# Two transformer layers on one core: V's high and low parts in one stationary tile, row sums spread by DMA, and an earlier place for the head products in cross-attention

## The chip, the core and the metric

The kernel runs on one core of one Trainium2 chip. Its engines work side by side, each through its own queue in order, and wait for each other through semaphores: TensorE (PE; matrix products into the eight PSUM banks, and transposes as products with the identity), VectorE (DVE), ScalarE (ACT), GpSimd (POOL), and SyncE (SP), which here issues every DMA. The metric is device time in microseconds. Lower is better.

## What is computed

A first layer (a gated state update with attention over a context) makes `x`, and a second layer, where most of the time goes, has three phases over 8 batches of 256 rows of 256 columns:

```python
h = layernorm(x, ln1_g, ln1_b)
x = attention(h, h, a1_Wq, a1_Wk, a1_Wv, a1_Wo, a1_bo) + x          # self
h = layernorm(x, ln2_g, ln2_b)
x = attention(h, context, a2_Wq, a2_Wk, a2_Wv, a2_Wo, a2_bo) + x    # cross, 120 rows of context
h = layernorm(x, ln3_g, ln3_b)
p = h @ ff_Wp + ff_bp
u, gate = jnp.split(p, 2, axis=-1)
return u * gelu(gate) @ ff_Wo + ff_bo + x

def attention(x, ctx, Wq, Wk, Wv, Wo, bo):       # 16 heads of 64
    sim = einsum('bihd,bjhd->bhij', q, k) / 8
    out = einsum('bhij,bjhd->bihd', softmax(sim), v)
    return out @ Wo + bo
```

## The kernel before

**High and low parts.** Products run in the type `F32R`, which keeps fewer bits than float32. So each operand is kept as two tiles: a rounded high part (written by ScalarE or GpSimd) and the low part that is left (a subtraction, nearly always on VectorE). A product is then three: high x high, low x high, high x low. The helper `product` issues them (L1386 to L1388).

**Steps.** The two attention phases run in 128 steps, one per batch and pair of heads: G = 8b + i, with i from 0 to 7, b from 0 to 7 for self-attention and 8 to 15 for cross-attention. Both heads of a pair (e = 0, 1) are worked together. The order on each engine is written out by hand in `step_self` and `step_cross`, one of each per engine, and a pipeline runs through them:

- `scores(G + 1)` on TensorE; `row_max` on VectorE; `softmax_pair` on ScalarE (exponentials, with their row sums to `expsum`); `inverse_sums` on VectorE gives `rs`, one reciprocal per row and head.
- `transpose_p(G)` on TensorE: the unscaled exponentials `p`, transposed into banks 4 and 5; `round_pT` (ScalarE) and `pT_low` (VectorE) write their high and low parts.
- `weighted_values(G - 1)` on TensorE, into bank 6: V (stationary) times pT (moving). The tiles `v_hi` and `v_lo` hold per pair [head 0 | zeros | head 1] of 64 columns each, so that each head's 128-column window puts the other head's 64 output rows to zero and both heads add up in one 128 x 256 result. That is 2 heads x 3 products x 2 tiles of rows in self-attention (12), x 1 in cross-attention (6). GpSimd had written the zeros once (L544 ff.).
- The scale by the row sums: `widen_sums` (GpSimd, L566) repeats the reciprocals over 64 columns, TensorE transposes that in two instructions into bank 6's right half (L1663), `copy_rT` (ScalarE, L781) copies it to SBUF, and `normalise_o` (VectorE, L1178) multiplies. Only then is bank 6 free for the next step.
- `split_o` (GpSimd) makes high and low parts of the scaled result, and `project_out` multiplies eight pairs by Wo into bank 7.

Between these stand the projections of later steps (`project_self`, `project_keys`, `project_queries`, `project_values`), and on fixed steps the preparation of the next batch: statistics at i = 0, `xhat` at 1, the residual of the batch before at 2, transposing and splitting the input at 3. In cross-attention the next batch's context is transposed at the end of step 3 (`context`), split at the start of VectorE's step 4 (`context_low`), and used by `project_keys(b + 1, 0)` in TensorE's step 4. New weights come in units of 1024 columns, one per step: in batch 0, the last self batch (7), the first cross batch (8) and the last (15).

**The changed places on TensorE:** in cross-attention a step is `scores`, `transpose_p`, a projection, `weighted_values`, then the rest (L1807 ff.).

## Time and profile before

| | us |
|---|---|
| median of 3 runs | 1027.96 (1027.17 to 1029.55) |
| profiled execution | 1026.68 |
| its span | 1024.9 |
| mean granted TensorE clock | 0.981 |
| TensorE / VectorE / ScalarE / GpSimd busy | 981.0 / 704.5 / 624.1 / 366.3 |

The span is the time from the first to the last instruction of the profiled execution; its own time is 1.8 us longer. Until 164.6 us runs mainly the first layer, then self-attention to about 576.9, cross-attention to about 874, and the feed-forward to the end. A timeline row gives the start, then the duration (for several instructions in a row, that of all). Matmuls are pipelined: a product of 256 columns is shown with 0.28 us but the next starts before its end, so the spacing of starts tells what one costs. L-numbers are lines of the kernel.

### The profile page before, as it was taken

The page shows a single profiled execution, that of the slowest core. Times are in us where ns is not written, and L with a number is a line of the kernel's source. Part 1 is how long each engine was busy: PE and PEld are TensorE (multiplying, and loading weights), DVE is VectorE, ACT ScalarE, POOL GpSimd, SP SyncE. Part 2 cuts the span into 40 slices and gives each one's busy share as a digit, 9 for nine tenths or more (in the row PEclk, how much of TensorE's full clock was granted, in tenths as well). Part 3 has the DMA queues.
Part 4 walks back from the last instruction along what each step waited for, and adds up shares of the span by engine and source line. Part 5 has one row for each costly group of instructions (what it writes and reads, how often), then busy time and mean ns, then how long its engine had stood idle before and what let it go on. Part 6 is the DMA issues. An engine that isn't in the chain of part 4 may idle for free.

```text
span 1024.9 us, 21429 instructions
## 1 busy us (share of the span) xinstructions
PE 981.0 (96%) x7892; PEld 921.9 (90%) x7892; DVE 704.5 (69%) x1594; ACT 624.1 (61%) x1945; POOL 366.3 (36%) x514
## 2 busy tenths in 40 slices
PE   7799999999999999999999999999999997999998
PEld 6687877899999999999999989999999997999998
DVE  5577578767676767676778777667667667566674
ACT  5556457757575756565667676676666667433343
POOL 1222337433333333342423345455454545301010
PEclk9799899999999999999999989999999999999999
DMA  7311100104000000000003000200000001001010
GB/s 219 102 42 42 36 21 32 32 2 104 2 22 1 23 1 22 2 21 2 22 2 88 21 27 23 87 27 27 2 27 26 2 22 62 22 22 38 26 32 22
DMA packets 30445, 34.62 MB, mean 34 GB/s; under 512 B 4360, under 2 KB 23816, under 8 KB 30344
## 3 DMA queue, kind: packets, MB, share of 16 engines
q1 hardware_dynamic: 30344, 33.26, 10.7%
q8 instruction: 65, 1.06, 0.4%
q14 instruction: 36, 0.29, 0.1%
HBM read 24.86 MB, written 8.39 MB: 32 GB/s over the span
## 4 chain that ended last, share of the span: by engine, by line
PE 81%; DVE 8%; ACT 7%; issue 2%; POOL 1%; SPq 0%; DMA 0%; DVEq 0%; ACTq 0%
PE bank L1386 15%; PE bank L1388 14%; PE bank L1387 14%; PE bank L1647 8%; PE bank L1626 5%; PE bank L1403 5%; PE bank L1689 3%; PE bank L1691 3%; PE bank L1690 3%; PE bank L1663 3%; ACT p L769 2%; PE bank L1508 1%; PE bank L1509 1%; PE bank L1510 1%; DVE hT_lo L1142 1%
## 5 line engine op out<-in xcount | busy, mean ns | idle before, releaser
L577 POOL TENSOR_TENSOR oT_hi<-oT,ones 128x256 fp32r<-128x256 f32 x128 | 93.9, 733 | 362.7 <-DVE oT L1182 362.7
L769 ACT ACTIVATE p<-bank,negmax 128x256 f32<-128x256 f32 (+1 forms) x512 | 207.8, 427 | 20.2 <-DVE negmax L1159 15.9
L779 ACT CAST pT_hi<-bank 128x512 fp32r<-128x512 f32 (+1 forms) x256 | 110.7, 486 | 166.6 <-PE bank L1647 166.4
L1386 PE MATMUL bank<-hT_hi,w_hi 128*128 128x256 f32 x640 | 188.5, 295 | 3.9 <-DVE qkT_lo L1213 1.6
L1388 PE MATMUL bank<-hT_hi,w_lo 128*128 128x256 f32 x640 | 179.0, 280 | 0.0
L1387 PE MATMUL bank<-hT_lo,w_hi 128*128 128x256 f32 x640 | 178.9, 280 | 0.0
L1174 DVE TENSOR_TENSOR pT_lo<-bank,pT_hi 128x512 fp32r<-128x512 f32 (+1 forms) x256 | 129.6, 547 | 0.5
L1155 DVE TENSOR_REDUCE negmax<-bank 128x2 f32<-128x512 f32 x128 | 82.1, 683 | 66.9 <-PE bank L1626 66.9
L1386 PEld LDWEIGHTS bank<-hT_hi,w_hi 128*128 128x128 f32 x640 | 121.6, 190 | 7.0 <-issue 3.6
L1387 PEld LDWEIGHTS bank<-hT_lo,w_hi 128*128 128x128 f32 x640 | 121.4, 190 | 0.0
L1388 PEld LDWEIGHTS bank<-hT_hi,w_lo 128*128 128x128 f32 x640 | 121.0, 189 | 0.0
L1386 PE MATMUL bank<-pT_hi,v_hi 128*128 128x256 f32 (+1 forms) x384 | 119.4, 311 | 0.0
L769 ACT ACTIVATION_READ_ACCUMULATOR p<-bank,negmax 128x1 f32 x512 | 110.2, 215 | 0.0
L1647 PE MATMUL bank<-ident,p 128*128 128x128 f32 (+1 forms) x768 | 109.9, 280 | 0.0
L1387 PE MATMUL bank<-pT_lo,v_hi 128*128 128x256 f32 (+1 forms) x384 | 108.7, 283 | 0.0
L1388 PE MATMUL bank<-pT_hi,v_lo 128*128 128x256 f32 (+1 forms) x384 | 108.6, 283 | 0.0
L579 POOL TENSOR_TENSOR oT_lo<-oT,oT_hi 128x256 fp32r<-128x256 f32 x128 | 94.6, 739 | 10.0
L1647 PEld LDWEIGHTS bank<-ident,p 128*128 128x128 f32 (+1 forms) x768 | 84.6, 141 | 8.7 <-ACT p L769 0.3
L568 POOL TENSOR_TENSOR rsum_wide<-rsum,ones 128x256 f32<-128x256 f32 x128 | 79.8, 624 | 0.0
L873 ACT ACTIVATE p<-bank,params_pp 128x256 f32<-128x256 f32 x64 | 30.4, 475 | 78.4 <-PE bank L1388 78.3
L1387 PEld LDWEIGHTS bank<-pT_lo,v_hi 128*128 128x128 f32 (+1 forms) x384 | 73.7, 192 | 0.0
L1388 PEld LDWEIGHTS bank<-pT_hi,v_lo 128*128 128x128 f32 (+1 forms) x384 | 73.4, 191 | 0.0
(204 smaller groups left out, 2738.9 us busy)
## 6 DMA issues: line engine op xcount, KB each, us to landing
w_stage<-in_weights SPq DMA_DIRECT2D x47, 256.0 KB, 4.6
x_in<-x_dram SPq DMA_DIRECT2D x24, 256.0 KB, 2.9
x_dram<-x_out SPq DMA_DIRECT2D x16, 256.0 KB, 3.2
l_x<-in_x SPq DMA_DIRECT2D x4, 512.0 KB, 5.0
x_dram<-l_out SPq DMA_DIRECT2D x4, 512.0 KB, 2.8
out_dram<-x_out SPq DMA_DIRECT2D x8, 256.0 KB, 3.1
w_stage<-in_weights SPq DMA_DIRECT2D x9, 128.0 KB, 5.6
l_ctx<-in_ctx SPq DMA_DIRECT2D x4, 180.0 KB, 4.4
```

Source lines behind the costliest of these rows:

```text
L568: nc.gpsimd.tensor_tensor(rsw[:, G % 2, :, :].rearrange("p t (e d) -> p (t e) d", e=2), rs[:, G % 2, :].unsqueeze(2).broadcast_to([128, NT ...
L577: nc.gpsimd.tensor_tensor(oh[:, G % PAIRS, :], of[:, :], ones[:, :], ALU.mult).then_inc(y["o_hi"], 1)
L579: nc.gpsimd.tensor_tensor(ol[:, G % PAIRS, :], of[:, :], oh[:, G % PAIRS, :].bitcast(F32), ALU.subtract).then_inc(y["o_lo"], 1)
L769: last = nc.scalar.activation(p[:, G % 2, e, t * cols:(t + 1) * cols], scores_at(G, e, t), ACT.Exp, bias=negmax[:, G % 2, t, e:e + 1], acc ...
L779: nc.scalar.copy(pTh[0:r, G % 2, e, 0:n], bank[4 + e][0:r, 0:n]).then_inc(y["pT_hi"], 1)
L1155: nc.vector.tensor_reduce(negmax[:, G % 2, :, e], score_bank(G, e)[:, :].rearrange("p (t n) -> p t n", t=NT), AX.X, ALU.max, negate=True). ...
L1174: nc.vector.tensor_tensor(pTl[0:r, G % 2, e, 0:n], bank[4 + e][0:r, 0:n], pTh[0:r, G % 2, e, 0:n].bitcast(F32), ALU.subtract).then_inc(y[" ...
L1386: nc.tensor.matmul(dst, lh, rh, start=(i == 0), stop=False)
L1387: nc.tensor.matmul(dst, lh, rl, start=False, stop=False)
L1388: last = nc.tensor.matmul(dst, ll, rh, start=False, stop=(i == n - 1))
L1403: last = nc.tensor.matmul(dst, *((a, c) if weights_stay else (c, a)), start=(i == 0), stop=(i == 4))
L1647: last = nc.tensor.transpose(bank[4 + e][0:n, j * S + t * 128:j * S + (t + 1) * 128], p[:, G % 2, e, t * cols + j * 128:t * cols + j * 128 ...
```

## The change

1. **One V tile.** `v_hi_lo` holds per head 128 columns: head 0 as [high | low], head 1 as [low | high]. One stationary load gives both products with high and low V; with pT's high and low parts that is 2 products per head and tile in place of 3 (the product low x low is now in). The zeros and their memsets go.
2. **Two halves to add.** Each head now has its own 128 x 256 half of a bank, 64 rows of high-V and 64 of low-V results. ScalarE copies the low-V rows to `oT_low_values` in two instructions of 64 x 256 (`copy_low_values`, in place of `copy_rT`), and VectorE adds them to the others in two (`add_low_values`, in place of `normalise_o`).
3. **Sums by DMA.** `widen_sums`, its two transposes and the copy go. SyncE writes the 512 reciprocals of a step to DRAM in 8-byte pieces (`send_sums`) and one step later reads them back, each head's row to 64 partitions (`spread_sums`). GpSimd multiplies the sum of halves by them, ahead of its two splitting instructions. Rings of four (`DEEP`) hold `oT` and `rsumT`.
4. **SyncE's queue** is written step by step: sends and spreads, with `load`, `store`, `load_context` and the weight units at fixed steps between them. A row `x_in` is loaded two batches ahead, not three.
5. **Cross-attention's order.** On TensorE `weighted_values(G - 1)` moves ahead of `transpose_p(G)`; its result alternates between banks 2 and 6 (`o_bank`), and scores use two banks, not three. On ScalarE the copies stand ahead of `round_pT` and the exponentials, on VectorE the additions ahead of `pT_low`. Both heads' transposed exponentials share one bank, so `round_pT` and `pT_low` are one instruction each.

```diff
-VW = 3 * DH
+VW = 2 * DH
+DEEP = 4
...
         def score_bank(G, e):
-            return bank[(2 * G + e) % 3 if G < STEPS // 2 else G % 3]
+            return bank[(2 * G + e) % 3 if G < STEPS // 2 else G % 2]
+        def o_bank(G):
+            return bank[6 if G < STEPS // 2 or G % 2 else 2]
+        def pT_both(G):
+            return bank[4 + G % 2][0:SC, :].rearrange("p (e n) -> p e n", e=2)
...
+            def send_sums(G):
+                sp.wait_ge(y["rsum"], G + 1)
+                if G >= DEEP:
+                    sp.wait_ge(*spread_until(G - DEEP))
+                sp.dma_start(sums_dram[G % DEEP, :, :].rearrange("e (q t) -> q e t", t=NT),
+                             rs[:, G % 2, :].rearrange("q (e t) -> q e t", e=2)).then_inc(y[f"rsum_row{G % 2}"], 16)
+            def spread_sums(G):
+                sp.wait_ge(y[f"rsum_row{G % 2}"], 16 * (G // 2 + 1))
...
+                for e in range(2):
+                    sp.dma_start(rT[e * DH:(e + 1) * DH, G % DEEP, :],
+                                 sums_dram[G % DEEP, e:e + 1, :].partition_broadcast(DH)).then_inc(y[f"rT{G % 2}"], 16)
...
             def split_o(G):
+                pool.wait_ge(y["o_sum"], G + 1)
+                pool.wait_ge(*spread_until(G))
...
+                nc.gpsimd.tensor_tensor(on[:, :].rearrange("p (t q) -> p t q", t=NT),
+                                        of[:, G % DEEP, :].rearrange("p (t q) -> p t q", t=NT),
+                                        rT[:, G % DEEP, :].rearrange("p (q t) -> p t q", t=NT),
+                                        ALU.mult).then_inc(y["o_norm"], 1)
...
-            def copy_rT(G):
+            def copy_low_values(G):
                 act.wait_ge(y["o"], G + 1)
-                nc.scalar.copy(rT[:, :], bank[6][:, S:2 * S]).then_inc(y["rT_copied"], 1)
+                if G >= 2:
+                    act.wait_ge(y["o_sum"], G - 1)
+                nc.scalar.copy(ob[0:DH, G % 2, :], o_bank(G)[DH:128, 0:S])
+                nc.scalar.copy(ob[DH:128, G % 2, :], o_bank(G)[0:DH, S:2 * S]).then_inc(y["o_low"], 1)
...
             def inverse_sums(G):
                 dve.wait_ge(y["exp"], 2 * G + 2)
+                if G >= 2:
+                    dve.wait_ge(y[f"rsum_row{G % 2}"], 16 * (G // 2))
...
-            def normalise_o(G):
+            def add_low_values(G):
+                dve.wait_ge(y["o_low"], G + 1)
+                if G >= DEEP:
+                    dve.wait_ge(y["o_norm"], G - DEEP + 1)
+                nc.vector.tensor_tensor(of[0:DH, G % DEEP, :], o_bank(G)[0:DH, 0:S], ob[0:DH, G % 2, :],
+                                        ALU.add)
+                nc.vector.tensor_tensor(of[DH:128, G % DEEP, :], o_bank(G)[DH:128, S:2 * S], ob[DH:128, G % 2, :],
+                                        ALU.add).then_inc(y["o_sum"], 1)
...
             def weighted_values(G):
+                    pe.wait_ge(y["o_sum"], G if G < STEPS // 2 else G - 1)
                 pe.wait_ge(y["pT_lo"], 2 * G + 2)
                 pe.wait_ge(y["v_lo"], values_until(b, g))
-                product(bank[6][:, 0:S], terms).then_inc(y["o"], 1)
+                for e in range(2):
+                    dst = o_bank(G)[:, e * S:(e + 1) * S]
+                    for j in range(tiles):
+                        vs = vv[0:r, j, (2 * g + e) * VW:(2 * g + e + 1) * VW]
+                        pc = slice(j * S, (j + 1) * S)
+                        nc.tensor.matmul(dst, vs, pTh[0:r, G % 2, e, pc], start=(j == 0), stop=False)
+                        last = nc.tensor.matmul(dst, vs, pTl[0:r, G % 2, e, pc], start=False, stop=(j == tiles - 1))
...
                 if G + 1 < STEPS:
                     scores(G + 1)
+                weighted_values(G - 1)
                 transpose_p(G)
...
-                weighted_values(G - 1)
```

**Three places in the instruction order**, each before and after. TensorE, cross-attention, from the last score product of step 3 on. `p` are the exponentials, `w,cT` is `project_values`, `pT,v` is `weighted_values`. Before:

```order
L1388 MATMUL bank<-qkT_hi,qkT_lo 128x240
L1647 MATMUL bank<-ident,p 120x128 x4
L1403 MATMUL bank<-w_hi,cT_hi 120x512
L1403 MATMUL bank<-w_hi,cT_lo 120x512
L1403 MATMUL bank<-w_lo,cT_hi 120x512
L1403 MATMUL bank<-w_hi,cT_hi 120x512
L1403 MATMUL bank<-w_lo,cT_hi 120x512
L1663 MATMUL bank<-ident,rsum_wide 128x128 x2
L1386 MATMUL bank<-pT_hi,v_hi 128x256
L1387 MATMUL bank<-pT_lo,v_hi 128x256
L1388 MATMUL bank<-pT_hi,v_lo 128x256
```

After:

```order
L1446 MATMUL bank<-qkT_hi,qkT_lo 128x240
L1733 MATMUL bank<-pT_hi,v_hi_lo 128x256
L1734 MATMUL bank<-pT_lo,v_hi_lo 128x256
L1733 MATMUL bank<-pT_hi,v_hi_lo 128x256
L1734 MATMUL bank<-pT_lo,v_hi_lo 128x256
L1713 MATMUL bank<-ident,p 120x128 x4
L1461 MATMUL bank<-w_hi,cT_hi 120x512
L1461 MATMUL bank<-w_hi,cT_lo 120x512
L1461 MATMUL bank<-w_lo,cT_hi 120x512
L1461 MATMUL bank<-w_hi,cT_hi 120x512
L1461 MATMUL bank<-w_lo,cT_hi 120x512
```

The products of `weighted_values` now stand ahead of the transposes, four in place of six, and the two `rsum_wide` transposes are gone.

VectorE, cross-attention, all of step 3 and the start of step 4 up to `context_low` (`cT_lo`, and the second instruction on `cT_hi`). `xhat<-bank` is the scaled input of the next batch, `oT<-bank,rsumT` is `normalise_o`. Before:

```order
L1167 RECIPROCAL rsum<-expsum 128x4
L1159 TENSOR_REDUCE negmax<-bank 128x4
L1136 TENSOR_SCALAR xhat<-bank,params_pp 128x256 x2
L1174 TENSOR_TENSOR pT_lo<-bank,pT_hi 120x256 x2
L1142 TENSOR_TENSOR hT_lo<-xhat,hT_hi 128x512
L1219 TENSOR_TENSOR v_lo<-bank,v_hi 120x4x2x64
L1182 TENSOR_TENSOR oT<-bank,rsumT 128x256
L1167 RECIPROCAL rsum<-expsum 128x4
L1159 TENSOR_REDUCE negmax<-bank 128x4
L1147 TENSOR_TENSOR cT_lo<-bank,cT_hi 128x120
L1148 TENSOR_TENSOR cT_hi<-bank,cT_hi 64x120
```

After:

```order
L1216 RECIPROCAL rsum<-expsum 128x4
L1206 TENSOR_REDUCE negmax<-bank 128x4
L1183 TENSOR_SCALAR xhat<-bank,params_pp 128x256 x2
L1237 TENSOR_TENSOR oT<-bank,oT_low_values 64x256
L1239 TENSOR_TENSOR oT<-bank,oT_low_values 64x256
L1229 TENSOR_TENSOR pT_lo<-bank,pT_hi 120x2x256
L1189 TENSOR_TENSOR hT_lo<-xhat,hT_hi 128x512
L1277 TENSOR_TENSOR v_hi_lo<-bank,v_hi_lo 120x4x128
L1216 RECIPROCAL rsum<-expsum 128x4
L1206 TENSOR_REDUCE negmax<-bank 128x4
L1194 TENSOR_TENSOR cT_lo<-bank,cT_hi 128x120
L1195 TENSOR_TENSOR cT_hi<-bank,cT_hi 64x120
```

`normalise_o` at the end of the step became two additions ahead of `pT_lo`, which is one instruction now.

ScalarE, cross-attention, steps 3 and 4 up to the exponentials. Before:

```order
L779 CAST pT_hi<-bank 120x256 x2
L769 ACTIVATE p,expsum<-bank,negmax 128x120 x4
L757 CAST hT_hi<-xhat 128x512
L801 CAST v_hi<-bank 120x4x2x64
L783 COPY rsumT<-bank 128x256
L761 CAST cT_hi<-bank 128x240
L779 CAST pT_hi<-bank 120x256 x2
L769 ACTIVATE p,expsum<-bank,negmax 128x120 x4
L783 COPY rsumT<-bank 128x256
```

After:

```order
L829 COPY oT_low_values<-bank 64x256
L830 COPY oT_low_values<-bank 64x256
L822 CAST pT_hi<-bank 120x2x256
L809 ACTIVATE p,expsum<-bank,negmax 128x120 x4
L797 CAST hT_hi<-xhat 128x512
L848 CAST v_hi_lo<-bank 120x4x2x64
L801 CAST cT_hi<-bank 128x240
L829 COPY oT_low_values<-bank 64x256
L830 COPY oT_low_values<-bank 64x256
L822 CAST pT_hi<-bank 120x2x256
L809 ACTIVATE p,expsum<-bank,negmax 128x120 x4
```

The one copy late in a step became two at its head, so that the rounding of pT and the exponentials stand behind them.

## Rows read from the trace of the kernel before

**Rows 1.** the profile page, busy time, share of the span and instructions by engine

```profile
PE 981.0 (96%) x7892; PEld 921.9 (90%) x7892; DVE 704.5 (69%) x1594; ACT 624.1 (61%) x1945; POOL 366.3 (36%) x514
```

**Rows 2.** windows: length, busy us (instructions) by engine, clock, DMA; self, cross, last cross batch

```profile
319.10:370.50 51.40, 51.40 (x444) 47.60 (x443) 35.02 (x73) 32.80 (x101) 18.11 (x27) 1.00 0.04 12
703.20:739.90 36.70, 35.54 (x299) 34.59 (x298) 26.00 (x65) 24.72 (x100) 18.34 (x27) 1.00 0.06 19
838.00:874.00 36.00, 30.18 (x225) 28.72 (x224) 25.11 (x58) 23.89 (x91) 16.27 (x23) 0.91 0.14 45
```

**Rows 3.** timeline: start us, us, line; TensorE in a self-attention step

```profile
301.31 0.28 PE L1388 MATMUL bank<-hT_hi,w_lo 128*128 128x256 f32 x1
301.44 0.38 PE L1663 MATMUL bank<-ident,rsum_wide 128*128 128x128 f32 x2
...
301.77 0.28 PE L1387 MATMUL bank<-pT_lo,v_hi 128*128 128x256 f32 x1
301.89 0.28 PE L1388 MATMUL bank<-pT_hi,v_lo 128*128 128x256 f32 x1
```

**Rows 4.** timeline of TensorE, cross batch 11, steps 2 to 5

```profile
703.22 0.60 PE L1647 MATMUL bank<-ident,p 128*120 128x128 f32 x4
...
712.26 0.41 PE L1663 MATMUL bank<-ident,rsum_wide 128*128 128x128 f32 x2 [1.16 <-DVE oT L1182]
...
713.29 0.32 PE L1403 MATMUL bank<-cT_hi,w_hi 128*128 128x120 f32 x1
...
716.30 0.60 PE L1647 MATMUL bank<-ident,p 128*120 128x128 f32 x4
```

**Rows 5.** timeline of VectorE over the same steps

```profile
706.17 0.69 DVE L1213 TENSOR_TENSOR qkT_lo<-bank,qkT_hi 128x512 fp32r<-128x512 f32 x1 [0.70 <-ACT qkT_hi L797]
...
707.36 0.66 DVE L1159 TENSOR_REDUCE negmax<-bank 128x4 f32<-128x480 f32 x1
707.93 0.99 DVE L1136 TENSOR_SCALAR xhat<-bank,params_pp 128x256 f32<-128x256 f32 x2
708.83 0.75 DVE L1174 TENSOR_TENSOR pT_lo<-bank,pT_hi 120x256 fp32r<-120x256 f32 x2
710.07 1.11 DVE L1142 TENSOR_TENSOR hT_lo<-xhat,hT_hi 128x512 fp32r<-128x512 f32 x1 [0.49 <-ACT hT_hi L757]
711.11 0.68 DVE L1219 TENSOR_TENSOR v_lo<-bank,v_hi 120x512 fp32r<-120x512 f32 x1
711.71 0.41 DVE L1182 TENSOR_TENSOR oT<-bank,rsumT 128x256 f32<-128x256 f32 x1
712.04 0.16 DVE L1167 RECIPROCAL rsum<-expsum 128x4 f32<-128x4 f32 x1
712.12 0.62 DVE L1159 TENSOR_REDUCE negmax<-bank 128x4 f32<-128x480 f32 x1
712.66 0.27 DVE L1147 TENSOR_TENSOR cT_lo<-bank,cT_hi 128x120 fp32r<-128x120 f32 x1
```

**Rows 6.** groups by line and shape: busy us, mean ns | idle before, releaser

```profile
L577 POOL TENSOR_TENSOR oT_hi<-oT,ones 128x256 fp32r<-128x256 f32 x128 | 93.9, 733 | 362.7 <-DVE oT L1182 362.7
...
L783 ACT COPY rsumT<-bank 128x256 f32<-128x256 f32 x128 | 49.5, 386 | 7.0 <-PE bank L1388 1.1
...
L324 DVE TENSOR_TENSOR w_lo<-w_stage,w_hi 128x1024 fp32r<-128x1024 f32 x22 | 27.0, 1229 | 17.0 <-ACT w_hi L314 17.0
...
L792 ACT CAST qkT_hi<-bank 64x480 fp32r<-64x480 f32 x32 | 17.7, 554 | 12.7 <-PE bank L1403 12.5
```

**Rows 7.** DMA issues by tile: KB each, median us from issue to landing

```profile
w_stage<-in_weights SPq DMA_DIRECT2D x47, 256.0 KB, 4.6
...
ctx_in<-in_ctx SPq DMA_DIRECT2D x8, 30.0 KB, 3.2
```

**Rows 8.** windows around a fall of the granted clock

```profile
596.80:600.40 3.60, 1.36 (x11) 1.27 (x12) 3.56 (x10) 2.23 (x10) 1.35 (x2) 1.00 0.59 180
600.40:607.20 6.80, 6.80 (x34) 6.80 (x34) 3.47 (x8) 3.98 (x13) 2.72 (x5) 0.50 0.01 2
```

201 lines of the change are left out of this document (107 added, 94 removed).

## The prediction, made before the change was timed

> **What bounds the kernel now.** I read the busy times first: TensorE is busy 96% of the span, VectorE 69%, ScalarE 61%, GpSimd 36% [rows 1]. Then the same by batch in the two attention phases (eight head pairs, one step each; this is what repeats). A self-attention batch takes 51.5 us and TensorE is busy in all of it. A cross-attention batch takes 36.7 us with TensorE busy 35.5 [rows 2]. So self-attention is bound by TensorE instruction for instruction, and cross-attention nearly. Third, TensorE's own rows in a cross batch: the one place where it waits is for `normalise_o`, 1.16 us, ahead of the `rsum_wide` transposes at 712.26 [rows 4]. Fourth, VectorE's rows over the same stretch explain that wait: from step i = 2 to i = 4 it has a chain with hardly a gap, and `normalise_o` stands near its end [rows 5]. I write T2 for the start of `transpose_p` in step i = 2 (703.22), T5 for that of i = 5 (716.30), and so on.
>
> **Self-attention, TensorE.** Back-to-back products of 256 columns start 0.12 us apart. From the last projection (301.31) over the two `rsum_wide` transposes and the first V product to the second (301.77) it is 0.46 us, where two plain intervals would be 0.24 [rows 3]. So the two transposes cost 0.22. Each step loses them and 4 of its 12 V products, which ran in intervals of 0.118 (0.12 rounded up): 0.22 + 4 x 0.118 = 0.69 us, 5.5 per batch, 44 over 64 steps if all of it shows.
>
> Does VectorE keep up? A batch has 35.0 us of VectorE work [rows 2]. In place of one multiply per step (0.41 us) come two additions on 64 partitions. Half the partitions do not mean half the time: ScalarE takes 0.55 us for 64x480 and 0.39 for 128x256 [rows 6], so time goes by elements per partition. Back to back, an instruction starts some 0.08 us ahead of its forerunner's shown end (the multiply at 711.71 takes 0.41, the next starts at 712.04 [rows 5]), so one more adds 0.33: 37.7 us. With a wait of some 0.7 per step for ScalarE's rounding of q and k, as at 706.17 [rows 5], it is 43.3 against TensorE's new 51.5 - 5.5 = 46.0. It fits, narrowly: steps 2 and 3, which also carry the residual and the next batch's input, I expect to run 1 us late and to be caught up by step 5. ScalarE makes two copies of 0.39 in place of one, 0.31 more back to back, 2.5 per batch: from 32.8 to 35.3. GpSimd swaps its widening for a multiply, so that it has three instructions of 0.73 a step [rows 6], 17.6 of 46: hidden.
>
> The cover is gone where weights are converted: a unit costs VectorE 1.23 us [rows 6]. Batch 0 has three units, the last self batch six, which brings VectorE there to 43.3 + 7.4, about 51. I take a gain of 4 us for batch 0, 1.5 for the last and 5.5 for each of the six between: 38.5.
>
> **Cross-attention.** On TensorE each step loses 2 of 6 V products and the transposes: 0.22 + 2 x 0.118 = 0.46. With the V products ahead of `transpose_p`, and two output banks, the wait for `normalise_o` goes. What is late next is the context: `project_keys` of the next batch cannot start before VectorE has `cT_lo`. That came at the end of the chain from 706.17 (queries' low part) to 712.66 and its second half, and the keys followed at 713.29 [rows 4, 5]: 7.1 us.
>
> I worked this chain again in the new order, start to start from the same rows: queries' low 0.61, reciprocal 0.08, row maximum 0.57, scaled input 0.90, additions 0.66, pT low 0.60 (now one instruction, as large per partition as the v_lo row), input low 0.78 to 1.04, v low 0.60, reciprocal 0.08, maximum 0.54, context 0.55. That is 6.0 to 6.3 us. The two multiplies and the 0.49 us wait before `hT_lo` leave, two pairs of additions less one enter. But the chain begins 0.3 us later after T2, since ScalarE makes its two copies (0.7) ahead of the rounding, which used to start 0.42 after T2. Taking 6.2, the keys start 9.5 us after T2 instead of 10.1. Behind them stand 20 short products (713.29 to about 715.57: 2.3), the scores 0.55 and now the V products 0.55, then T5: 12.9 against 13.1 before. I take 0.3 gained in these three steps. TensorE sits idle in them in four pieces (at the values, the context, the V products, the keys), 2.7 us together, the longest 1.7.
>
> The other five steps are TensorE's own: 0.46 each in four, and 0.2 in step 1, where `project_queries` waits for `keys_low`, now later. Per batch 0.3 + 4 x 0.46 + 0.2 = 2.35. Six even batches give 14. The first, with two weight units in this very stretch, I take at 2; the last, where five units bind VectorE and ScalarE already (TensorE 30.2 of 36.0 [rows 2]), at 0.5. Cross-attention together 16.6.
>
> **The sums by DMA.** No row shows a transfer in 8-byte pieces, 256 to a step. The nearest are 30 KB in 256-byte pieces, 3.2 us to landing, and the 256 KB parts of weight units, 4.6 [rows 7]. With 3.2 the spread of pair G-1, issued about 1.4 us after the reciprocal of step G, lands at 4.6; GpSimd needs 2.2 more, 6.8; the tightest user, pair 7 in `project_out` of cross step 1, asks at about 7.9: 1.1 to spare. A landing time of 4.6 would eat 1.4: 0.3 us at step 1, 2 us in all. A gain it cannot be, since the transposes it replaces are already counted. I take 0, by the nearest row. VectorE's new wait (the reciprocal of G on the send of G-2) has two steps, 9 us; behind it queue the row maximum and with it the exponentials. Between the sends SyncE now has single loads and stores, each waiting for what was done a step before; only `store_first(3)` at G = 1 holds the next send, until GpSimd's last pass over the first layer, and pair 2's sum is not wanted before that pass is over. Cost 0.
>
> The Trainium skill speaks against this part: "DMA: Bandwidth & Descriptors", Specifications, has pieces under 512 B handled by read-modify-write, and its account of the fixed cost of about 2 us says that completion waits for the memory written, HBM worst. No row here shows such writes; by that page alone two trips of 2 us would still fit in the 4.6.
>
> **Edges.** The removed memsets stood on GpSimd beside a busy TensorE: 0. At the start of the feed-forward, pair 127's split has a third instruction ahead of `project_out`: 0.7 lost. And the clock. The granted clock is 1.00 in even batches [rows 2], but 0.50 (the 1.2 GHz level) from 600.4 to 607.2, right behind 3.6 us in which TensorE was busy 1.36 [rows 8]. The idle that I expect ahead of T5 comes close to that in some batches: I charge 2 us. The Trainium skill ("TensorE: Matmul & The Clock Gate", Part 1) has the clock set by how busy the array has lately been; the trace agrees at 600.4.
>
> **Sum.** 38.5 + 16.6 - 0.7 - 2 = 52.4. The profiled execution took 1026.7 us (span 1024.9 and 1.8 around it); the median shown, 1028.0, is 1.3 above. 1026.7 - 52.4 + 1.3 = 975.6. I say 975, its own range 966 to 985.
>
> **Rivals.**
> 1. TensorE binds everywhere: 64 x 0.69 + 64 x 0.46, and the wait of 1.2 in seven batches: 44 + 29 + 8 = 81, 947 us. For it: the busy share of 96%. Against it: VectorE's chain, whose parts are all in one queue. Chance 0.12.
> 2. Self-attention becomes bound by VectorE and ScalarE. If the lateness in steps 2 and 3 reaches `project_values(b, 3)`, which asks for `v_lo` within 0.1 us of when I have it, or additions cost more than 0.33, half of 38.5 is lost: 994 us. For it: 43.3 of 46.0 leaves little. Against: ScalarE's part of the wait shrinks when VectorE is late. Chance 0.14.
> 3. The clock falls in nearly every cross batch. A fall lasts 6.8 us at half speed [rows 8], of which waiting hides a part; at 2.4 us a batch the 16.6 are gone: 992 us. For it: idle of 2.7 us ahead of T5. Against: the present wait never did it in an even batch. Chance 0.12.
> 4. The sums' round trip binds, and it is slower than before. A send is waited for two steps later, so a send of L us forces steps of at least L/2. Steps now average 6.4 and 4.6 [rows 2]; with L = 12 cross steps take 6.0 (64 x 1.4 = 90 us more) and self-attention keeps some 28 of its gain: 1090 us. It turns the change into a loss from about L = 10.5, where cross steps lose 39. For it: 256 tiny writes, in no row. Against: nothing in [rows 7] is near. Chance 0.03.
>
> Forecast 0.59. The range 957 to 997 takes in rivals 2 and 3 at their price and stops short of 1 and 4. A measurement of this kernel tells 0.2%, 2 us, from no change: faster 0.95, same 0.02, slower 0.03.
>
> **What the profile after would show.** A self batch of 46.0 us with TensorE busy throughout; above 47 it is rival 2. A cross batch of 34.3, with TensorE waiting at `project_keys` for `cT_lo` and at the V products for `pT_lo`; 33 or less, or 36, and my chain is wrong. Granted clock 1.00 in even batches, else rival 3. Additions at 0.41 us, copies at 0.39. Sends landing within 5 us, and VectorE never waiting at the reciprocal, else rival 4.

## The result, and the profile after

The changed kernel takes **1004.68 us** (median of 4 runs, 1004.02 to 1005.22) against 1027.62 of the kernel before, run beside it: ratio 0.977 [0.976, 0.979]. I had forecast 975, between 957 and 997. The change is faster, by less than half of what I expected.

The busy times of the changed kernel; they answer to [rows 1]:

```profile
PE 931.9 (93%) x7252; PEld 864.4 (86%) x7252; DVE 768.2 (77%) x1658; ACT 672.5 (67%) x2009; POOL 388.3 (39%) x498
```

TensorE lost 49 us of work, 640 instructions, but the span lost only 21.9: TensorE now waits more. Where, by stretches of the span, T being the first `transpose_p` of a step:

| us | before | after | gained | forecast |
|---|---|---|---|---|
| to T of G = 0 | 164.6 | 163.9 | 0.6 | 0 |
| batch 0 | 51.3 | 50.9 | 0.4 | 4 |
| batches 1 to 6 | 51.54 each | 46.40 each | 30.9 | 33 |
| batch 7 (converts weights) | 51.8 | 55.6 | -3.8 | 1.5 |
| batch 8 | 43.0 | 41.2 | 1.8 | 2 |
| batches 9 to 14 | 36.67 each | 34.7 to 39.9 | -4.6 | 14.1, less 2 for the clock |
| batch 15, to T of G = 127 | 33.4 | 31.4 | 2.0 | 0.5 |
| from there to the end | 151.5 | 156.9 | -5.3 | -0.7 |

In the windows of the changed kernel (columns as in [rows 2]) the first row is a plain self batch, the second cross batch 9, the third cross batch 11, the fourth batches 9 to 14 together:

```profile
307.60:354.00 46.40, 46.33 (x399) 42.37 (x397) 39.78 (x81) 35.88 (x109) 19.68 (x27) 1.00 0.15 36
590.03:624.73 34.70, 32.52 (x267) 30.84 (x266) 28.52 (x66) 27.43 (x100) 19.86 (x26) 1.00 0.45 110
661.44:701.36 39.92, 37.06 (x267) 35.41 (x266) 29.32 (x66) 27.73 (x100) 19.91 (x27) 0.87 0.19 44
...
590.03:814.63 224.60, 207.98 (x1586) 197.77 (x1585) 174.97 (x391) 165.54 (x600) 119.02 (x157) 0.94 0.24 56
```

The same six batches in the kernel before:

```profile
619.93:839.95 220.02, 213.06 (x1779) 207.36 (x1778) 155.97 (x390) 148.33 (x600) 109.82 (x157) 1.00 0.09 28
```

Read the clock's column first. It was 1.00 in all six and is 0.94. TensorE was busy 213.1 us with 1779 instructions and is busy 208.0 with 1586: a tenth of the instructions gone, a fortieth of the time. Batches 9 and 11 hold the same 267 products, and in batch 11 they take 4.5 us more. Only batch 9 had no fall of the clock.

The same columns for the stretch just before the fall in batch 11 and for the fall itself, which is at half clock (the 1.2 GHz level); they answer to [rows 8]:

```profile
678.66:680.50 1.84, 0.61 (x6) 0.36 (x4) 1.84 (x5) 1.32 (x3) 1.69 (x3) 0.99 0.06 20
680.50:690.70 10.20, 9.64 (x45) 9.64 (x46) 5.52 (x13) 5.24 (x21) 3.83 (x6) 0.50 0.32 67
```

and TensorE's rows there, steps 3 to 5 of batch 11 (answering to [rows 4]). The wait ahead of the keys is the last bracket; the products behind it, 120 columns each, start 0.21 us apart:

```profile
675.13 0.46 PE L1461 MATMUL bank<-w_hi,cT_hi 128*120 128x512 f32 x1 [0.27 <-DVE qkT_lo L1271]
...
678.11 0.36 PE L1733 MATMUL bank<-pT_hi,v_hi_lo 120*128 120x256 f32 x1 [0.43 <-issue]
678.66 0.60 PE L1713 MATMUL bank<-ident,p 128*120 128x128 f32 x4
681.06 0.47 PE L1461 MATMUL bank<-cT_hi,w_hi 128*128 128x120 f32 x1 [1.79 <-DVE cT_hi L1195]
681.32 0.42 PE L1461 MATMUL bank<-cT_lo,w_hi 128*128 128x120 f32 x1
681.54 0.42 PE L1461 MATMUL bank<-cT_hi,w_lo 128*128 128x120 f32 x1
```

In batch 9 the same wait is 1.12 us and the keys start 9.52 us after T2, T5 follows 13.0 after T2:

```profile
599.45 0.60 PE L1713 MATMUL bank<-ident,p 128*120 128x128 f32 x4
...
608.97 0.32 PE L1461 MATMUL bank<-cT_hi,w_hi 128*128 128x120 f32 x1 [1.12 <-DVE cT_hi L1195]
612.47 0.38 PE L1713 MATMUL bank<-ident,p 128*120 128x128 f32 x2
```

### The profile page after: what moved, and what is told of

It reads as the page before. It is cut to its first block, busy times and chain, and to the rows that moved or that the text cites. A ratio compares the mean times of both kernels' runs of the same rounds, so it can differ in the third digit from the quotient of the medians.

```text
span 1002.9 us, 21207 instructions
## 1 busy us (share of the span) xinstructions
PE 931.9 (93%) x7252; PEld 864.4 (86%) x7252; DVE 768.2 (77%) x1658; ACT 672.5 (67%) x2009; POOL 388.3 (39%) x498
## 4 chain that ended last, share of the span: by engine, by line
PE 70%; DVE 13%; ACT 9%; issue 4%; DMA 2%; POOL 1%; SPq 1%; DVEq 0%; POOLq 0%
PE bank L1444 10%; PE bank L1445 9%; PE bank L1446 9%; PE bank L1461 5%; PE bank L1704 5%; PE bank L1684 5%; PE bank L1733 4%; PE bank L1734 4%; ACT p L809 3%; PE bank L1752 3%; PE bank L1754 3%; PE bank L1753 3%; PE bank L1713 1%; PE bank L1566 1%; PE bank L1567 1%
## 5 line engine op out<-in xcount | busy, mean ns | idle before, releaser
L613 POOL TENSOR_TENSOR oT_scaled<-oT,rsumT 128x256 f32<-128x256 f32 x128 | 98.2, 767 | 318.6 <-DVE oT L1239 177.4
L1444 PEld LDWEIGHTS bank<-hT_hi,w_hi 128*128 128x128 f32 x640 | 123.3, 193 | 13.1 <-issue 10.2
L1733 PE MATMUL bank<-pT_hi,v_hi_lo 128*128 128x256 f32 (+1 forms) x384 | 102.2, 294 | 14.8 <-DVE oT L1239 4.9
L1734 PE MATMUL bank<-pT_lo,v_hi_lo 128*128 128x256 f32 (+1 forms) x384 | 100.1, 289 | 0.0
L618 POOL TENSOR_TENSOR oT_hi<-oT_scaled,ones 128x256 fp32r<-128x256 f32 x128 | 95.3, 745 | 10.0
L620 POOL TENSOR_TENSOR oT_lo<-oT_scaled,oT_hi 128x256 fp32r<-128x256 f32 x128 | 94.3, 737 | 10.0
L1733 PEld LDWEIGHTS bank<-pT_hi,v_hi_lo 128*128 128x128 f32 (+1 forms) x384 | 75.5, 197 | 17.9 <-DVE oT L1239 9.7
L1224 DVE TENSOR_TENSOR pT_lo<-bank,pT_hi 128x512 fp32r<-128x512 f32 x128 | 81.9, 681 | 0.0
L1752 PE MATMUL bank<-w_hi,oT_hi 128*128 128x256 f32 x256 | 73.5, 287 | 4.4 <-POOL oT_lo L620 4.4
L1734 PEld LDWEIGHTS bank<-pT_lo,v_hi_lo 128*128 128x128 f32 (+1 forms) x384 | 75.7, 197 | 0.0
L1753 PE MATMUL bank<-w_lo,oT_hi 128*128 128x256 f32 x256 | 71.6, 280 | 0.0
```

The lines of the kernel that those rows point to most:

```text
L613: nc.gpsimd.tensor_tensor(on[:, :].rearrange("p (t q) -> p t q", t=NT), of[:, G % DEEP, :].rearrange("p (t q) -> p t q", t=NT), rT[:, G % ...
L618: nc.gpsimd.tensor_tensor(oh[:, G % PAIRS, :], on[:, :], ones[:, :], ALU.mult).then_inc(y["o_hi"], 1)
L620: nc.gpsimd.tensor_tensor(ol[:, G % PAIRS, :], on[:, :], oh[:, G % PAIRS, :].bitcast(F32), ALU.subtract).then_inc(y["o_lo"], 1)
L1444: nc.tensor.matmul(dst, lh, rh, start=(i == 0), stop=False)
L1733: nc.tensor.matmul(dst, vs, pTh[0:r, G % 2, e, pc], start=(j == 0), stop=False)
L1734: last = nc.tensor.matmul(dst, vs, pTl[0:r, G % 2, e, pc], start=False, stop=(j == tiles - 1))
```

## The experiments

Sixteen kernels, each with its own runs of the kernel before beside it. Each edit is to the changed kernel. Medians and ratios are of all its runs; the last two columns are of its one profiled execution, which was the slowest of its kernel's in e8, e12, e13 and e17 and the fastest in e4, e10, e14 and e16. Transposes called "idle" compute nothing that is read.

| | us | ratio to before | batches 9 to 14, us | falls in them, us at half clock |
|---|---|---|---|---|
| changed | 1004.7 | 0.977 [0.976, 0.979] | 224.6 | 5, 27.2 |
| e1_weights_last | 1003.2 | 0.976 [0.972, 0.980] | 221.0 | 4, 20.4 |
| e2_fill14 | 988.8 | 0.962 [0.959, 0.964] | 210.9 | 0 |
| e3_early_w24 | 1000.0 | 0.975 [0.971, 0.978] | 219.2 | 3, 17.0 |
| e7_old_cross_order | 1034.0 | 1.006 [1.004, 1.007] | 246.4 | 6, 40.8 |
| e8_no_sums | 997.0 | 0.969 [0.965, 0.973] | 223.0 | 5, 30.6 |
| e4_vlow_later | 999.0 | 0.972 [0.969, 0.975] | 218.5 | 4, 20.4 |
| e9_cut_unit_lo | 1003.2 | 0.975 [0.971, 0.978] | 225.3 | 4, 23.8 |
| e10_fill_ends | 992.2 | 0.965 [0.962, 0.968] | 213.4 | 0 |
| e12_fill_vlow | 992.1 | 0.963 [0.959, 0.967] | 219.0 | 2, 6.8 |
| e13_fill7 | 997.0 | 0.971 [0.967, 0.975] | 221.3 | 4, 17.0 |
| e14_cut_units | 999.7 | 0.972 [0.970, 0.975] | 224.8 | 5, 34.0 |
| e15_up_first | 990.1 | 0.962 [0.958, 0.966] | 213.1 | 0 |
| e16_spread_loads | 993.8 | 0.965 [0.962, 0.968] | 212.6 | 0 |
| e17_fill10 | 985.1 | 0.956 [0.954, 0.959] | 210.8 | 0 |
| e18_bias_late | 985.0 | 0.958 [0.956, 0.959] | 211.8 | 1, 3.4 |
| e19_short_chain | 998.9 | 0.972 [0.970, 0.973] | 219.1 | 3, 17.0 |

**The clock.** e2 puts work where TensorE waits ahead of the keys: transposes of the identity into the score bank that is free there.

```diff
             def step_cross(G):   # TensorE, behind transpose_p(G)
+                if i == 4 and more:
+                    for n in range(14):
+                        nc.tensor.transpose(score_bank(G, 0)[:, n % 4 * 128:(n % 4 + 1) * 128], ident[:, :], ident[:, :])
```

> The changed kernel, with 14 transposes of the identity on TensorE in cross step 4 of batches 8 to 14, behind transpose_p and ahead of project_keys, where TensorE waits about 1.8 us for cT_lo. They write a scores bank whose contents are used up. Theory A (the granted clock): five of the six even cross batches took 36.7 to 39.9 us with a fall to 0.50 beside project_keys, the sixth 34.7 without one. With TensorE active over the wait the clock stays at 1.00, all six take 34.7 to 35.0, and the time falls by 14 to 17 us, to 988 to 991. Rival B (the spread between batches comes from DMA traffic, or from VectorE's lateness): the added work does nothing or costs up to 0.2 us a batch, 1004 to 1006, and batches keep their spread.

Batches 9 to 14 of e2, and TensorE at the fourth step of its batch 11:

```profile
588.77:799.65 210.88, 203.72 (x1670) 194.19 (x1669) 173.23 (x391) 164.99 (x600) 118.44 (x156) 1.00 0.26 60
```

```profile
675.63 0.60 PE L1713 MATMUL bank<-ident,p 128*120 128x128 f32 x4
676.06 1.69 PE L1879 MATMUL bank<-ident 128*128 128x128 f32 x14
```

More instructions than in the changed kernel (1670 against 1586), less busy time (203.7 against 208.0), the clock 1.00, 13.7 us less in the six batches. Theory A holds: keeping the clock up by filling is worth that, and the total of 988.8 is in its range.

e13 takes 7 transposes in place of 14.

> As e2, with 7 idle transposes in step 4 of the even cross batches in place of 14. Theory A, how much of the idle stretch is filled decides how often the clock falls: some falls come back, one to three batches of 36.5 or more, 990 to 998. Rival B, any work in that place is enough: no fall in the even batches, 34.7 to 35.3 each, 985 to 988.

Four falls in three batches; 35.3 to 35.5 in the three without. Half the filling was not enough (A), though the two falls of batch 10 go with a late row sum (below), so two batches of one profile, and the median of 997.0, carry this.

Shortening the wait instead: e4 moves `values_low(b, 1)` on VectorE from the end of step 3 to step 4, behind `context_low`.

```diff
                 if i == 4 and more:
                     context_low(b + 1)
+                if i == 4:
+                    values_low(b, 1)
...
-                if i == 3:
-                    values_low(b, 1)
```

> In cross-attention the low part of V's second half leaves VectorE's step 3 for step 4, behind the context's low part. The chain ahead of the next keys is 0.6 us shorter. Theory A, the fall of the clock is set off by TensorE's waiting in front of the keys: with 0.6 us less of it there are fewer falls, step 4 is 5.2 or less wherever no fall comes, and the six even batches sum up to 210 or less (they were 224.6): 990 to 994. Rival B, the idle that counts stands elsewhere (in front of the values or the context): step 4 gains at most 0.6 us where no fall comes, falls come as often, 1000 to 1004.

Rival B, by its falls and its gain per step, with a total (999.0) 1 us under its range: step 4 gained its 0.6 where the chain met nothing else (4.59 in batch 12, against 5.22 in batch 9 of the changed kernel, both without a fall), and falls still came in four batches. There is a second effect, which lengthens the wait from batch to batch. Summed from TensorE's rows, its waits from T2 to the keys are 1.16 us in every batch of the kernel before, but 1.87 (batch 9), 2.26, 2.55, 2.85, 2.03 and 2.57 in the changed one. The differences are those of one VectorE instruction, `hT_lo`. Batch 9 and batch 11:

```profile
606.52 0.68 DVE L1189 TENSOR_TENSOR hT_lo<-xhat,hT_hi 128x512 fp32r<-128x512 f32 x1
...
677.92 1.36 DVE L1189 TENSOR_TENSOR hT_lo<-xhat,hT_hi 128x512 fp32r<-128x512 f32 x1
679.21 0.68 DVE L1277 TENSOR_TENSOR v_hi_lo<-bank,v_hi_lo 120x512 fp32r<-120x512 f32 x1
```

GpSimd in the same two places:

```profile
606.57 1.22 POOL L618 TENSOR_TENSOR oT_hi<-oT_scaled,ones 128x256 fp32r<-128x256 f32 x1
...
677.46 1.28 POOL L604 TENSOR_TENSOR x_plus_bias<-x_in,rows_bc 128x512 f32<-128x512 f32 x1
```

Where `x_plus_bias` was under way first (677.46), `hT_lo` ends 0.5 us behind it and takes 1.36; where `hT_lo` was first, by 0.05, GpSimd's instruction takes 1.22 in place of 0.74. `v_hi_lo`, with one operand from a bank, takes 0.68 in both. The Trainium skill ("SBUF — State Buffer", SBUF: two separate sides) says that a VectorE instruction with two inputs from SBUF and a GpSimd instruction that reads SBUF shut each other out for the whole instruction; the rows agree, except that `hT_lo` ends 0.54 to 0.56 us behind `x_plus_bias` in all five batches where that came first, a little less than its own 0.68. When `x_plus_bias` comes depends on when GpSimd got the row sums, so on the DMA: in e8 (below), which has no sums, it came 4.5 us after T2 in all six batches and `hT_lo` took 0.72 or 0.73.

That does not settle where the clock falls. In e8 TensorE's waits from T2 to the keys were 1.82 to 1.86 us in all six batches, less than in batch 9 of the changed kernel, and five of the six had a fall; batch 14 of e3 had 2.41 and none. Batch 9 of e8, VectorE, TensorE at the keys, and the fall:

```profile
607.34 0.72 DVE L1189 TENSOR_TENSOR hT_lo<-xhat,hT_hi 128x512 fp32r<-128x512 f32 x1
```

```profile
609.83 0.32 PE L1461 MATMUL bank<-cT_hi,w_hi 128*128 128x120 f32 x1 [1.15 <-DVE cT_hi L1195]
```

```profile
610.70:617.50 6.80, 6.80 (x34) 6.80 (x33) 3.19 (x7) 2.93 (x9) 2.19 (x3) 0.50 0.12 37
```

So the lengthening adds to the wait, but why one batch falls and its equal does not stays open.

e18 (from e17, below) moves `x_plus_bias` behind step 4's split in cross-attention, and the load of its row one step later.

```diff
-                if i == 3:
+                if i == 3 and b < B:
                     add_bias(b + 1)
                 if G >= 1:
                     split_o(G - 1)
+                if i == 4 and b >= B:
+                    add_bias(b + 1)
```

> As e17, with GpSimd's x_plus_bias in cross-attention behind the split of step 4 in place of ahead of that of step 3 (and the row's load one step later). In the profiles so far VectorE's hT_lo in step 3 takes 0.68 us when x_plus_bias runs elsewhere and 0.8 to 1.7 when the two meet. Theory A, this meeting is what lengthens the chain ahead of the keys now and then: hT_lo 0.68 to 0.73 in every even batch, step 4 at 5.15 to 5.25 in each (5.15 to 5.75 in e17), 981 to 984. Rival B, GpSimd's other instructions meet it as much, or VectorE's in step 4 are lengthened in place: no batch gains, 984 to 987.

`hT_lo` took 0.68 or 0.69 in all six batches and step 4 took 4.91 or 4.92 in five (5.15 to 5.75 in e17). A holds for the chain, and the gain in step 4 is larger than I said. The whole did not gain: the median is 985.0 against e17's 985.1, in B's range. In the profiled execution (989.2) batch 10 lost 4.1 us to a late row sum.

e19 has both moves, e4's and e18's, and no idle transposes.

> No idle transposes at all: the changed kernel with V's second low part in step 4 (as e4) and x_plus_bias behind step 4's split (as e18), so that TensorE's waits between T2 and the keys should add up to 1.25 us in every even batch (1.16 in the kernel before, 1.9 to 2.9 in the changed one). Theory A, the clock falls because of that waiting, however it is taken away: falls in at most one even batch, these at 34.1 to 34.4 each, 984 to 989. Rival B, only work in the place of the waits holds the clock: falls in three or more of the six, 995 or more.

The total, 998.9, is B's; the falls are neither's. The waits were 1.26 to 1.54 and three falls came in two batches, two of them in batch 10 with its late row sum (42.4 us). Of the five other batches one had a fall (waits 1.40), where four of five had one in the changed kernel; the best took 34.06. So shortening the wait removed most of the falls that come without a late sum, and does not make it safe.

**The order in cross-attention.** e7 puts the head products, the copies and the additions back where they stood before, on all three engines, and keeps the rest.

```diff
             def step_cross(G):   # TensorE; the copies and additions likewise to the end of ScalarE's and VectorE's step
-                weighted_values(G - 1)
                 transpose_p(G)
...
                     project_queries(b + 1, i - 5)
+                weighted_values(G - 1)
```

> The changed kernel with the order of cross-attention as it was before: weighted_values behind transpose_p and the projection, copies and additions at the end of ScalarE's and VectorE's steps. One V tile, sums by DMA, two output banks and the merged rounding stay. Theory A (the new order sets up the clock falls: it puts the output products ahead, so TensorE stands idle in one piece ahead of project_keys): the old order has the output products to fill this wait, fewer falls, cross batches of 35 to 36 us and 3 to 10 us less in all, 995 to 1002. Rival B (the new order helps, as forecast): batches of 37 us or more without regard to the clock, and 5 to 10 us more, 1010 to 1015.

Rival B, and more than that: slower than the kernel before. VectorE's rows in its batch 9 show why. At the end of the step the additions stand ahead of the next reciprocal and row maximum, and the exponentials wait for these:

```profile
608.16 0.42 DVE L1237 TENSOR_TENSOR oT<-bank,oT_low_values 64x256 f32<-64x256 f32 x1
608.59 0.43 DVE L1239 TENSOR_TENSOR oT<-bank,oT_low_values 64x256 f32<-64x256 f32 x1
609.04 0.18 DVE L1216 RECIPROCAL rsum<-expsum 128x4 f32<-128x4 f32 x1
609.25 0.66 DVE L1206 TENSOR_REDUCE negmax<-bank 128x4 f32<-128x480 f32 x1
```

The keys start 11.6 us after T2 in that batch, and TensorE's waits up to there add up to 3.7 (4.2 to 4.7 in the next five); a fall came in every batch. With the V tile and the sums by DMA the new order is needed, not an extra: it is worth 29 us (1034.0 against 1004.7).

**Self-attention's weight batches.** e1 puts copies and additions ahead of the units' conversions on ScalarE and VectorE.

```diff
             def step_self(G):    # ScalarE; add_low_values likewise on VectorE
+                if G >= 1:
+                    copy_low_values(G - 1)
                 if b == 0 and i in (0, 2, 4):
                     weights_hi(act, 9 + i // 2)
...
-                if G >= 1:
-                    copy_low_values(G - 1)
```

> The changed kernel, but in self-attention ScalarE's copy_low_values and VectorE's add_low_values stand ahead of the weight units and of zero_keys, not behind them. Theory A (the queue order makes the additions late: a unit of 1.07 us on ScalarE and 1.23 us on VectorE stands between the output products and the additions, and the next reciprocal, row maximum and the next output products in bank 6 wait behind them): batch 0 gets 3 to 4 us back of the 4.5 it lacks, the last self batch 4 to 7 of the 9.2 it lacks, together 7 to 11 us, time 994 to 998. Rival B (the sum of VectorE's work in these batches binds, in whatever order): 0 to 2 us, 1003 to 1005.

Batches 0 and 7 took 51.5 and 55.0 (50.9 and 55.6): rival B, the order does not matter. e9 and e14 convert 64 of each unit's 1024 columns, on VectorE alone, then on both engines; the rest of these weights is left out, so this is for the time only.

```diff
             def weights_lo / weights_hi, units 9 to 17
+            dst, src, hi = dst[:, :, 0:32], src[:, :, 0:32], hi[:, :, 0:32]
```

> The low parts of weight units 9 to 17 are computed for 64 of 1024 columns, so VectorE's 1.23 us per unit shrinks to about 0.15 in the first and last self batch; ScalarE's conversions stay. Theory A, VectorE is what these steps wait for: batch 0 falls from 50.9 to 48 and batch 7 from 55.6 to 50, 994 to 996 in all. Rival B, ScalarE's 1.07 us in front of its copies is: less than 3 us come back in the two together, 1001 or more.

> Units 9 to 17 are converted for 64 of 1024 columns on both engines, so ScalarE's 1.07 and VectorE's 1.23 us per unit shrink to 0.2 or less. Theory A, the conversions alone are what the first and last self batch lose: batch 0 at 47 (one gap of layer one kept), batch 7 at 46.5 to 48. Rival B, something else stands there (the first layer's last tasks in batch 0, the units' DMA and the cleared key tiles in batch 7): batch 0 above 48.5, batch 7 above 49.5.

| us | batch 0 | batch 7 |
|---|---|---|
| changed | 50.9 | 55.6 |
| VectorE's part cut | 49.5 | 51.9 |
| both cut | 47.3 | 50.7 |

The conversions cost 3.6 of the 4.5 us by which batch 0 is above 46.4, 1.4 of it through VectorE's part alone; in batch 7 4.9 of 9.2, 3.7 through VectorE's. So e9 lies between its theories, nearer to A in batch 7; its total, 1003.2, is B's. In its profile 5.1 us came back in the two batches and 3.6 were lost elsewhere (1.1 ahead of batch 0, 1.5 in batch 8, which had a fall of 10.2, the rest in the even batches and at the end). e14 is theory A in batch 0 and rival B in batch 7. The rest of batch 7 I put down to the turn to cross-attention, which no run takes away: in e14 steps 5 to 7 took 9.58, 6.43 and 6.00, where plain batches take 5.75, 5.69 and 6.43, so most of the excess is in step 5. It has the first cross keys (20 products, their rounding on ScalarE, two memsets and their low part on VectorE), and a fall of the clock. In e14 the even cross batches took 224.8: what was gained here left the clock as it was.

**The sums by DMA.** e8 leaves the sends and spreads out, so that nothing is divided by the row sums.

```diff
-                send_sums(G)
-                if G >= 1:
-                    spread_sums(G - 1)
...
+                nc.gpsimd.memset(rT[:, :, :], 1.0).then_inc(y["rT0"], 1)
```

> Leaves out the division by the row sums: no send, no spread, GpSimd multiplies by ones. TensorE, VectorE and ScalarE do what they did. Theory A, the sums' DMA costs nothing anywhere but behind the last pair: self batches 46.4 and T127 within 1 us of the changed kernel where the clock falls alike (846), the stretch after T127 shorter by 2 to 5 us, 1000 to 1003 in all, and step 3 of a self batch still 6.00. Rival B, GpSimd's waits for the spread or VectorE's for the send delay others in the steady steps: self step 3 back at 5.68 and cross batches shorter by over 0.5 each even at full clock, 990 or less.

Self step 3 stayed at 6.00, and the one cross batch without a fall took 34.7: in the steady steps the DMA makes no engine late by itself (A). It does move `x_plus_bias`, and with it `hT_lo`, as shown above. From T of G = 127 to the end it took 152.7 in place of 156.9. The median, 997.0, is 3 us under A's range and far from B's; the profiled execution (1000.5) is in A's range, and what the other three (992.3 to 999.2) gained, no profile shows. GpSimd's rows at the end of the changed kernel:

```profile
854.12 0.91 POOL L613 TENSOR_TENSOR oT_scaled<-oT,rsumT 128x256 f32<-128x256 f32 x1 [4.19 <-DMA rsumT<-rsums_dram]
...
856.92 1.39 POOL L613 TENSOR_TENSOR oT_scaled<-oT,rsumT 128x256 f32<-128x256 f32 x1 [0.28 <-DMA rsumT<-rsums_dram]
...
859.25 0.84 POOL L620 TENSOR_TENSOR oT_lo<-oT_scaled,oT_hi 128x256 fp32r<-128x256 f32 x1
```

TensorE stands at the last pairs' `project_out` for them (860.15, waited 2.48), and the clock is at half from 861.4 for 6.8 us. The send of G = 127 took 5.9 us to land; it was issued at 847.8 between two pairs of 256 KB loads.

Later profiles showed the same wait elsewhere: `project_out` of pair 7 in step 1, the "tightest user" of the prediction. In e12's batch 14 GpSimd, then TensorE, then the windows with the fall:

```profile
773.69 0.74 POOL L613 TENSOR_TENSOR oT_scaled<-oT,rsumT 128x256 f32<-128x256 f32 x1 [6.52 <-DMA rsumT<-rsums_dram]
...
776.71 0.74 POOL L613 TENSOR_TENSOR oT_scaled<-oT,rsumT 128x256 f32<-128x256 f32 x1
...
778.33 0.73 POOL L620 TENSOR_TENSOR oT_lo<-oT_scaled,oT_hi 128x256 fp32r<-128x256 f32 x1
```

```profile
779.11 0.54 PE L1756 MATMUL bank<-w_hi,oT_hi 128*128 128x256 f32 x1 [2.01 <-POOL oT_lo L620]
```

```profile
775.00:779.20 4.20, 2.19 (x17) 1.80 (x16) 4.01 (x8) 2.12 (x10) 3.82 (x6) 1.00 0.13 32
779.20:782.60 3.40, 3.40 (x16) 3.40 (x17) 0.51 (x1) 0.00 (x0) 2.19 (x3) 0.50 0.16 39
```

Step 1 took 9.03 us there and 9.58 in batch 10, in place of 4.88. In the changed kernel it cost 1.0, in batch 13; the most was 5.8, in batch 10 of e19, with a fall in it. e8 had none. e12 itself has 14 idle transposes in the even batches, 36 in the first, and e4's move:

> Idle transposes in cross step 4 (14 in even batches, 36 in the first, none at the ends), and VectorE's low part of V's second half behind the context's low part. Theory A, the idle transposes hold the clock and the shorter chain is then worth its 0.6 us in step 4: even batches 34.2 to 34.9 each, 982 to 986. Rival B, with 14 transposes step 4 is bound by them and not by the chain, or clock falls come back: even batches 35.3 or more, 987 or more.

Four batches without a late sum took 34.8 to 35.7, with 14 transposes holding step 4 at 5.35 or more: B. e16 keeps the transposes and asks whether the four weight units that SyncE issues in batch 9 are the cause; it loads them one per batch.

```diff
-                if b == B + 1 and i < 4:
-                    load_weights(sp, 20 + i, 21 + i)
+                if B + 1 <= b <= B + 4 and i == 2:
+                    load_weights(sp, 11 + b, 12 + b)
```

> Idle transposes as in e12 (14 and 36), V's low part in its old place, and the four weight units that SyncE loads in steps 0 to 3 of cross batch 9 are loaded one per batch, in step 2 of batches 9 to 12. Theory A, the loads crowd the sends: without them no send of batch 9 takes over 6 us (7 to 8.6 now), pair 7's sum is in time and step 1 of batch 10 takes 4.9 (6.9 to 9.6 in four of the runs with idle transposes), 983 to 987. Rival B, slow landings come by themselves: step 1 of some batch still takes over 6, 988 to 992.

The slowest send of batch 9 took 6.5 us (8.6 in e12, 7.3 in the changed kernel) and step 1 of batch 10 took 4.88. But batch 13's took 5.87, the total of 993.8 is above both ranges, and in e18, with the same loads, batch 10's took 8.33. So crowding is part of it, at the sends; the late sums also come without it, and what makes them late stays open.

**The ends.** Three tries to shorten the last stretch: units 24 and 25 loaded two steps earlier; idle transposes in the first and last cross batch and in the feed-forward; a block of up-projections ahead of the last `project_out`.

```diff
-                if b == 2 * B - 1 and i >= 6:
-                    load_weights(sp, 18 + i, 19 + i)
+                if b == 2 * B - 1 and i in (4, 5):
+                    load_weights(sp, 20 + i, 21 + i)
```

> The changed kernel, with the last two weight units (24, 25) issued at steps 4 and 5 of the last cross batch, not at 6 and 7. In the changed kernel unit 24 landed at 850.2, 2.4 us after ScalarE was ready for it, its table load and first gelu wait behind it, and the last row sums came 5.8 us after their issue with a unit issued around them. From the last transpose_p to the end it took 156.9 us, before 151.5. Theory A (late units and the sums queued with them cost this): the stretch gets 3 to 5 us shorter, 1000 to 1002. Rival B (the third GpSimd instruction and the clock fall at 861 cost it): under 1 us, 1004 to 1005.

```diff
+                if i == 4:
+                    keep_busy(score_bank(G, 0), 36 if b == B else 14 if more else 40)
...
-                            project_out(b - 1, 5, 8)
+                            project_out(b - 1, 5, 7)
+                            keep_busy(bank[5], 60)
+                            project_out(b - 1, 7, 8)
```

> Idle transposes as in e2 (14 in step 4 of the even cross batches), and also 36 in step 4 of the first cross batch, 40 in step 4 of the last and 60 in front of the last pair's project_out in the feed-forward. Theory A, the three falls that e2 kept (571.6, 820.8, 844.7; 24 us at half clock) cost what TensorE's own work in them takes longer: without them 976 to 983. Rival B, in these stretches TensorE waits for VectorE, ScalarE and the weights anyway, so the clock there costs nothing: 986 to 990 though the falls are gone.

```diff
-                    if j == 3:
+                    if j == (4 if it == 0 else 3):
                         if it == 0:
                             project_out(b - 1, 5, 8)
```

> e12, and in the feed-forward's first batch the fifth block of up-projections (24 products, 2.9 us) ahead of the last three pairs' project_out. Theory A, TensorE waits there for the last pairs' sums and GpSimd's splits, and the block fills that wait: the stretch behind the last transpose_p is 2 to 3.5 us shorter than in e12, 979 to 983. Rival B, the wait moves behind the block, since VectorE and ScalarE then do the residual late and the next batch's statistics with it: less than 1 us.

The last stretch took 155.9 (e3), 157.1 (e10) and 156.7 (e15, which has e12's edits too; e12 took 157.4). e3's total of 1000.0 is its theory A's, but by luck: the stretch gained 1.0 of the 3 to 5 us, and the even batches, which the edit does not touch, took 5.4 less. In e10 only 3.4 us at half clock were left in the stretch, and it was no shorter: TensorE waits for the others in it (B, though the total of 992.2 is above B's range). e15 gained less than 1 us (B). Only the first cross batch gained from its 36 transposes, 41.2 to 38.6.

**The best version.** e17 takes what worked: 10 idle transposes (30 in the first cross batch), e4's move, e16's and e3's loads.

> e16's loads, 10 idle transposes in even batches and 30 in the first, V's second low part in step 4, units 24 and 25 loaded two steps earlier. Theory A, with the shorter chain ten transposes fit into the wait: step 4 takes 5.0 to 5.2 in place of 5.35, no fall in the even batches, these at 34.3 to 34.8 each, 980 to 984. Rival B, ten are too few, as seven were in e13: one to three batches over 36, 986 or more.

985.1, 4.4% less than the kernel before and some 2% less than the changed one. The even batches were 34.7 to 35.9, no fall (near A, whose range ends at 984; the excess is `hT_lo` meeting `x_plus_bias`, and a late sum in batch 11):

```profile
656.79:692.64 35.85, 33.90 (x277) 32.02 (x276) 29.41 (x66) 27.48 (x100) 19.68 (x27) 1.00 0.31 68
692.64:727.35 34.71, 33.66 (x277) 32.04 (x276) 29.03 (x66) 27.47 (x100) 19.67 (x26) 1.00 0.29 66
```

## Why the prediction was wrong, step by step

The span gained 21.9 us where I had 52.4. The missing 30.5 lie in the even cross batches (16.7, most of it the clock), the two weight batches (8.9), the last stretch (4.6) and the plain self batches (2.1); the other stretches give 1.9 back.

- **Self-attention, TensorE: right.** 46.40 against 46.0. Seven steps a batch gained 0.63 to 0.70 (0.69 said). Step 3 gained 0.38: VectorE is busy 5.85 of its 6.00 us, and the lateness that I expected to be caught up stays as 0.3.
- **The weight batches: wrong by 9 us.** I counted VectorE's 7.4 us of conversions in batch 7 and took 51 as its load, and so as the batch's time; VectorE was busy 48.4 and the batch took 55.6, so engines waited for each other. I had left out ScalarE's 1.06 per unit, which stands in series with VectorE's 1.23 (without both, e14 got 4.9 back), and the turn's first cross keys. The rows of batch 7:

```profile
493.19:548.82 55.63, 48.39 (x395) 44.43 (x394) 48.43 (x91) 41.58 (x115) 19.95 (x28) 0.97 0.29 70
```

- **Cross-attention's chain: right in batch 9, and only there.** Keys 9.52 us after T2 (9.5 said), T5 at 13.0 (12.9), step 1 4.88 (0.12 less than before; 0.2 said), 34.69 per batch (34.3 said). My own 12.9 against 13.1 would have been 0.2 gained from T2 to T5, not the 0.3 that I summed; it was 0.06. In the other five the keys start 9.7 to 10.5 us after T2, since `hT_lo` varies (below). The rows show the order said: `cT_lo` and its second half the last release, TensorE's waits for it 12.7 us in seven batches:

```profile
PE bank L1461 <- DVE cT_hi L1195: 12.7, 7, 3.0
```

- **The clock: the step that failed.** I wrote "I charge 2 us", for idle that I had put at 2.7 us ahead of T5 myself. Six batches like batch 9 would take 208.1; they took 224.6. Of these 16.5, `hT_lo`'s lengthening is 2.9 and a late sum 1.0; the falls are the other 12.6, six times my charge, and e2 gave 13.7 back by filling alone. It is rival 3, to which I gave 0.12; its 2.4 us a batch were 2.1. Its argument against itself, "the present wait never did it", compared 1.16 us with 2.7. I should have taken rival 3 as the likeliest: it says 992, and with the weight batches and the end right, 1006; that this is so near 1004.7 is in part luck, since smaller errors cancel.
- **A term that I took as fixed.** My chain used 0.78 to 1.04 for `hT_lo`, from the 1.11 in [rows 5], where it met `x_plus_bias` (start 709.34, 1.29 us) in the same way in every batch. In the changed kernel it takes 0.68 alone and up to 1.66 when they meet. Over the even batches it took 7.0 us; by my term it is some 5.5, and by e8's 0.72, without the sums, 4.3. I had the sums at no cost.
- **The sums by DMA: no wait in most steps, but wrong at the edge and in step 1.** Sends land in 3.15 us (median of 128; 3.2 taken), nine over 5, the longest 7.3. VectorE's reciprocal waited for a send once, 0.59 us in batch 9. My tightest user, `project_out` in step 1, was late by 1.0 us in batch 13, and by up to 5.8 in later versions. Behind the last pair nothing hides the trip: 4.2 us by e8, in which the fall there was also 3.4 us long in place of 6.8. The stretch from there lost 5.3 where I had 0.7, all but 0.1 of it in the first feed-forward batch (the second batch's first `gelu` came 32.6 us after T of G = 127, 27.4 before).
- Additions took 0.41 and 0.43, copies 0.37 each (0.41 and 0.39 said), the adding of two per step no more than I had:

```profile
L1239 DVE TENSOR_TENSOR oT<-bank,oT_low_values 64x256 f32<-64x256 f32 x128 | 54.7, 428 | 1.7
L1237 DVE TENSOR_TENSOR oT<-bank,oT_low_values 64x256 f32<-64x256 f32 x128 | 52.9, 413 | 13.1 <-ACT oT_low_values L830 9.1
L829 ACT COPY oT_low_values<-bank 64x256 f32<-64x256 f32 x128 | 47.2, 369 | 54.3 <-PE bank L1734 52.5
```
